# An attention stage: the values product is taken two query tiles after the scores, spare score banks hold some projections, and the engines' orders are rewritten

## The reference

```
q_latent, kv_latent = x @ wq_down, x @ wkv_down          # ranks 192 and 64
q = [q_latent @ wq_nope, rope(q_latent @ wq_rope)]       # 16 heads, 128 + 64 wide
k = [kv_latent @ wk_nope, rope(kv_latent @ wk_rope)]
v = (kv_latent @ wv_up).reshape(b, t, 16, 192)
scores = einsum('bthd,bshd->bhts', q, k) / sqrt(192)     # causal mask, then softmax
out = einsum('bhts,bshd->bthd', softmax(scores), v).reshape(b, t, 16 * 192) @ wo
```

## Time and profile before

| | us |
|---|---|
| median of 3 runs (1310.30 to 1316.01) | 1311.97 |
| the profiled execution, its own time | 1314.4 |
| its span, first to last instruction | 1312.6 |
| PE / DVE / ACT / POOL busy over the span | 1161.8 / 720.3 / 646.2 / 493.9 |

### The profile page before, as it was taken

How to read it: one execution, slowest core, us unless ns; L and a number is a source line. 1 busy time by engine, 2 the same in 40 slices (tenths; PEclk the granted TensorE clock), 3 DMA queues, 4 the chain that set the end, 5 groups by cost and what they waited for, 6 DMA issues and landing times. The chain is left out here.

```text
span 1312.6 us, 23292 instructions
## 1 busy us (share of the span) xinstructions
PE 1161.8 (89%) x7616; PEld 936.2 (71%) x7616; DVE 720.3 (55%) x1298; ACT 646.2 (49%) x1287; POOL 493.9 (38%) x386
## 2 busy tenths in 40 slices
PE   6678889888888898898888988998999999999997
PEld 3456667667677676676776766776788887888886
DVE  6556756556555556565555565554444445444444
ACT  3545556555555565555555555664433333333332
POOL 1263534543444445335444453421333332333332
PEclk9989999999999999999999999998999999999999
DMA  5001001000000000100000000103633333533332
GB/s 194 33 0 32 1 1 32 1 0 26 5 0 2 28 0 0 31 0 0 31 0 0 15 0 1 57 25 97 198 112 115 112 114 107 143 114 111 113 112 88
DMA packets 26304, 67.35 MB, mean 51 GB/s; under 512 B 3029, under 2 KB 9557, under 8 KB 26265
## 3 DMA queue, kind: packets, MB, share of 16 engines
q1 hardware_dynamic: 26120, 66.78, 16.6%
q10 hardware_dynamic: 144, 0.07, 0.0%
HBM read 62.36 MB, written 4.47 MB: 51 GB/s over the span
## 5 line engine op out<-in xcount | busy, mean ns | idle before, releaser
L714 ACT ACTIVATE prob<-ps_s,nm 128x128 f32<-128x128 f32 (+7 forms) x256 | 189.5, 740 | 203.3 <-DVE nm L866 200.9
L1305 POOL TENSOR_TENSOR hl<-hf,hh 128x512 fp32r<-128x512 f32 x96 | 123.5, 1286 | 294.9 <-ACT hh L1242 294.9
L866 DVE TENSOR_REDUCE nm<-ps_s 128x1 f32<-128x128 f32 (+7 forms) x256 | 192.3, 751 | 70.5 <-PE ps_s L548 69.0
L571 PE MATMUL ps_o<-pt,kvn 128*64 128x128 f32 x2304 | 154.0, 277 | 64.5 <-DVE pt L875 49.5
L571 PEld LDWEIGHTS ps_o<-pt,kvn 128*64 128x64 f32 x2304 | 126.2, 136 | 100.9 <-ACT pt L724 51.2
L559 PE MATMUL ps_t<-ident,prob 128*128 128x128 f32 x1152 | 173.0, 276 | 9.4 <-DVE pt L875 6.7
L1017 POOL TENSOR_TENSOR xtf<-xtf,sinv 128x512 f32<-128x512 f32 x62 | 79.4, 1280 | 223.4 <-DVE xtf L835 221.2
L559 PEld LDWEIGHTS ps_t<-ident,prob 128*128 128x128 f32 x1152 | 138.7, 142 | 32.2 <-issue 10.9
L1032 POOL TENSOR_TENSOR qlo<-t,qhi 64x512 fp32r<-64x512 f32 x64 | 82.0, 1281 | 159.8 <-ACT qhi L751 147.2
L724 ACT ACTIVATE pt<-ps_t 128x128 f32<-128x128 f32 (+2 forms) x192 | 96.6, 503 | 88.1 <-PE ps_t L559 86.7
L875 DVE COPY pt<-ps_t 128x128 f32<-128x128 f32 (+2 forms) x192 | 101.6, 529 | 56.2 <-PE ps_t L559 55.3
(11 more groups left out here) (272 smaller groups left out, 2689.5 us busy)
## 6 DMA issues: line engine op xcount, KB each, us to landing
routing<-wT_scratch SPq DMA_DIRECT2D x34, 256.0 KB, 3.7
raw_a<-in_e SPq DMA_DIRECT2D x17, 384.0 KB, 3.1
cosv<-in_e SPq DMA_DIRECT2D x17, 384.0 KB, 3.1
sinv<-wT_scratch SPq DMA_DIRECT2D x17, 384.0 KB, 3.6
raw<-in_e SPq DMA_DIRECT2D x17, 384.0 KB, 3.0
routing<-wT_scratch SPq DMA_DIRECT2D x16, 384.0 KB, 3.3
raw_a<-in_a SPq DMA_DIRECT2D x8, 512.0 KB, 3.3
raw_b<-in_b SPq DMA_DIRECT2D x8, 480.0 KB, 3.9
```

The lines of the kernel that those rows point to most:

```text
L571: mm = nc.tensor.matmul(ps_o[64 * e:64 * e + 64, at], kvn[:, b * 8 + j, :], pt[t % 2][:, e, j, :], start=j == 0, stop=j == t)
L714: nc.scalar.activation(prob[t % 2][e][:, 0:len(halves) * width].rearrange("p (h k) -> p h k", k=width), ps_s[e][:, 0:len(halves), 0:width] ...
L866: nc.vector.tensor_reduce(out=nm[:, e:e + 1], in_=ps_s[e][:, 0:len(halves), 0:halves[0][1]], axis=AXXY, op=ALU.max, negate=True).then_inc( ...
L1305: nc.gpsimd.tensor_tensor(hl[:, c, :], hf[:, c, :], hh[:, c, :].bitcast(F32), ALU.subtract).then_inc(h_lo, 1)
```

## The change

PE takes V(t-2) in tile t where it took V(t-1). The lists of all four engines are rewritten around that. Lp and QR1 go to the second bank of head 0, and KR0 and KR1 to that of head 1 (`SPARE`), while tiles 0 to 3 leave these banks free; a later S(4,e) waits until DVE has read QR1 or KR1 there. The others stay in `ps_x`. Lp moves from tile 0 to tile 1, KR1 from 5 to 3, L0 from 4 to 5, Yp1 from 6 to 4, QL1 from the end of 5 into 6 ahead of V(4), B from the end of 6 to that of 5, WA from 7 to the end of 6. On POOL the difference pass of KR0 (L1032) now stands behind `out_low` of the round's first half, and that of KR1 still ends the round; ACT rounds KR1's rotated part (`rope_hi` with `which`) only in tile 1 of the next round. The amount of work is the same. Parts that only rename or pass a bank along are left out.

```diff
-STAGE = ["Lp", "QR0", "KR0", "QL0", "QR1", "L0", "Yp0", "KR1", "QL1", "Yp1", "B", "WA", "Y0", "Y1"]
+STAGE = ["QR0", "Lp", "KR0", "QL0", "QR1", "KR1", "Yp0", "Yp1", "L0", "B", "QL1", "WA", "Y0", "Y1"]
+TURNS = {"QR0": "W0", "KR0": "W1", "QL0": "W2", "QR1": "W3"}
+SPARE = {"Lp": 0, "QR1": 0, "W3": 0, "KR0": 1, "KR1": 1, "W1": 1}
...
+            return ps_s[SPARE[name]][:, 1, :] if name in SPARE else ps_x
...
-                return a_split, (0 if b is None else i + 1) * 4 + 4
+                return a_split, (0 if b is None else i + 1) * 4 + 2
...
+                if t == TPC and half == 1:
+                    held = ("KR1" if e else "QR1") if not is_last(i, b) else "W1" if e else "W3"
+                    pe.wait_ge(*consumed(i, b, held))
...
                         if t == 0:
                             scores(i, b, t, 0, 0)
-                            if has:
-                                turn(sp, tp, 0, 0)
-                                turn(sp, tp, 0, 1)
+                            turns(0)
+                            products()
                             scores(i, b, t, 1, 0)
+                            turns(1)
+                            also("QR0")
+                        elif t == 1:
+                            scores(i, b, t, 0, 0)
+                            products()
                             also("Lp")
...
+                            turns(0)
+                            turns(1)
+                            scores(i, b, t, 1, 0)
+                            also("KR0")
                         elif t < TPC:
                             scores(i, b, t, 0, 0)
-                            turn(sp, tp, 0, 0)
-                            turn(sp, tp, 1, 0)
+                            turns(0)
+                            also("QL0" if t == 2 else "QR1")
+                            products()
+                            turns(1)
                             scores(i, b, t, 1, 0)
-                            values(sp, bp, tp)
-                            also(("KR0", "QL0", "QR1")[t - 1])
+                            if t == 3:
+                                also("KR1")
                         elif t == TPC:
                             scores(i, b, t, 0, 0)
-                            turn(sp, tp, 0, 0)
                             scores(i, b, t, 0, 1)
-                            also("L0")
-                            turn(sp, tp, 1, 0)
+                            turns(0)
+                            also("Yp0")
+                            products()
+                            turns(1)
                             scores(i, b, t, 1, 0)
                             scores(i, b, t, 1, 1)
-                            values(sp, bp, tp)
-                            also("Yp0")
+                            also("Yp1")
                         else:
                             scores(i, b, t, 0, 0)
                             turn(sp, tp, 0, 0)
                             scores(i, b, t, 0, 1)
                             turn(sp, tp, 0, 1)
-                            also(("KR1", "Yp1", "WA")[t - TPC - 1])
-                            scores(i, b, t, 1, 0)
-                            turn(sp, tp, 1, 0)
-                            turn(sp, tp, 1, 1)
-                            scores(i, b, t, 1, 1)
+                            if t < TILES - 1:
+                                also(("L0", "QL1")[t - TPC - 1])
+                            products()
                             if t == TILES - 1:
                                 also("Y0")
-                            values(sp, bp, tp)
-                            also(("QL1", "B", "Y1")[t - TPC - 1])
+                            scores(i, b, t, 1, 0)
+                            turns(1)
+                            scores(i, b, t, 1, 1)
+                            also(("B", "WA", "Y1")[t - TPC - 1])
...
-                        rope_low(s + 1, 0, 1 - b, (rope_sum, s * 4 + 7))
-                        rope_low(s + 1, 1, 1 - b, (rope_sum, s * 4 + 7))
                         rope_sum_of(s + 1, 3)
+                        rope_low(s + 1, 0, 1 - b, (rope_sum, s * 4 + 8))
...
                     out_low(s, 0)
                     if more:
+                        rope_low(s + 1, 1, 1 - b, (olo_done, s * 2 + 1))
                         rope_low(s + 1, 2, 1 - b, (olo_done, s * 2 + 1))
                         rope_low(s + 1, 3, 1 - b, (olo_done, s * 2 + 1))
```

More of the change, by code:

```diff
@@ L332, in misc_predecessor @@
 def misc_predecessor(i, b, name):
[L334 to L340, removed]
+    spare = SPARE.get(name)
+    order = FIRST if isinstance(i, int) and i == 0 else LAST if isinstance(i, int) and i == PAIRS - 1 else LATER
+    if spare is not None:
+        earlier = [x for x in order[:order.index((b, name))] if x[0] == b and SPARE.get(x[1]) == spare]
+        return (i, *earlier[-1]) if earlier else None
+    earlier = [x for x in order[:order.index((b, name))] if x[1] not in SPARE]
+    if earlier:
+        return (i, *earlier[-1])
+    return (0, None, PROLOGUE[-1]) if isinstance(i, int) and i == 0 else (i - 1, *LATER[-1])
 def halves_of(t):
@@ L637, in body, with turns, products @@
                     for t in range(TILES):
-                        sp, bp, tp = before_tile(i, b, t)
-                        has = earlier or t > 0
+                        sp, _, tp = before_tile(i, b, t)
+                        def turns(e):
+                            if earlier or t > 0:
+                                for g in range(len(groups_of(tp))):
+                                    turn(sp, tp, e, g)
+                        def products():
+                            if earlier or t > 1:
+                                values(*before_tile(i, b, t, 2))
@@ L688, in _ @@
             s, t = 2 * PAIRS - 1, TILES - 1
-            for e in range(2):
-                for g in range(2):
-                    turn(s, t, e, g)
+            for g in range(2):
+                turn(s, t, 0, g)
+            values(s, 1, t - 1)
+            for g in range(2):
+                turn(s, t, 1, g)
             pe.wait_ge(widened, s * 2 + 2)
@@ L912, in body @@
                         has = earlier or t > 0
+                        if more and t == 1:
+                            rope_products(i, b, "QR0", s + 1)
+                        if more and t == 2:
+                            rope_products(i, b, "KR0", s + 1)
+                        if more and t == 3:
+                            latent_low(i, b, 0, s + 1, 1 - b)
+                        if more and t == TPC:
+                            rope_products(i, b, "KR1", s + 1)
+                        if t == TPC + 1 and earlier:
+                            add_out(misc(i, b, "Yp1"), ps_x, s - 1, 1 - b, 1, 1)
@@ L913, in body @@
+                        if t == TPC + 2 and b == 0:
+                            split_b(i, b)
+                        if t == TPC + 3 and b == 0 and not is_last(i):
+                            split_a(i, b, i + 1)
+                        maximum(s, t, 0)
+                        if has and (t == 0 or t > TPC):
+                            take_turned(sp, tp, 0, 1)
                         if t == 0 and earlier:
                             invert(s - 1, 1)
+                        if more and t == 3:
+                            rope_products(i, b, "QR1", s + 1)
@@ L929, in body @@
-                        if more and t == TPC + 1:
-                            rope_products(i, b, "KR1", s + 1)
-                        if t == TPC + 2 and earlier:
-                            add_out(misc(i, b, "Yp1"), ps_x, s - 1, 1 - b, 1, 1)
-                        if t == TPC + 3 and b == 0 and not is_last(i):
-                            split_a(i, b, i + 1)
-                        if has and t > TPC:
-                            take_turned(sp, tp, 1, 1)
-                        maximum(s, t, 1)
```

143 lines of the change are left out of this document (70 added, 73 removed).

## The result

The changed kernel takes 1193.26 us (median; 1190.07 to 1212.5), the kernel before 1311.13 on the same chip. The ratio is 0.909, with a 95% interval of 0.905 to 0.913; ratios leave out executions in a second, slower state, such as the one at 1212.5 here. The forecast was 1203, within 1180 to 1252. The profiled execution took 1190.85, its span is 1189.0.

A forecast was written before the change was run, and what follows sets the result against it. PE was held by late results, its waits worth 131 us; less 22 us left or new, 109 gained: 1205.4 in the profiled run's terms, 1203 in the median's. Forecast range 1180 to 1228 (0.68), wider range 1180 to 1252.

The forecast's parts named there:

- The bound and the floor: PE in attention rounds: late results, not engine time, bound it; all waits worth 131 us, floor 1183 in the profiled run.
- sign of being wrong: PE's busy time in a round not the same as before, or waits left over 4 us a round.
- V, spreads, Yp1: PE's waits for transposed copies, ACT's filling and QL1's bank all go: 75.4, 28.0 and 13.9 us.
- Transposes: PE's waits for copies to leave banks: of 13.8 us, 0.2 a round stays, at T(6,0) in tile 7.
- Tight places: S(4,0) fits with 0.4 us to spare, S(3,0) comes 0.3 late a round, Yp0 fits with 1.2.
- the 6 us allowed for errors of these chains: Places with under 0.5 us to spare: 0.4 a round allowed, 6 us.
- WA: Behind QL1 in its bank: waits 0.8 us in each of eight b = 0 rounds, 6.4 us.
- First and last rounds: These rounds have lists of their own; 2 us kept for them.
- Heads of line: Rival: lists stall as a whole, tight places come late, 47 us in fifteen rounds, 1250; chance 0.21.
- the 2.98 us: DVE's idle time for ACT ahead of reading QL0, with C(2,1) said to be ready behind it.
- Waits that only move: Rival: V's waits return at S, only the spreads' and Yp1's go, 42 us, 1270; chance 0.05.
- wait of PE was for POOL: Rival: late `out_low` holds PE at Yp0 and POOL sets the round; 1335 at 10 us late; slower 0.04.

The follow-up runs named there:

- tuned_unrolled: Changed kernel with three small moves on ACT and DVE, and the loop over the six middle pairs of rounds written out; 1176.42 us, ratio 0.8949.
- tuned: Changed kernel with E(2,0) ahead of tile 2's rounding, QL1's reading ahead of E(6,0), two of the first four rotation differences on DVE; 1191.88 us, ratio 0.9087.
- late_latent: Changed kernel with ACT's reading of QL0 cut from two copies into sixteen small ones; 1204.73 us, ratio 0.9189.
- lag_one: Changed kernel with V(t-1) again at the end of tile t, only V(0) staying in tile 2; 1312.29 us, ratio 0.9999.
- before_lag_banks: Kernel before with V(t-2) in tile t and Lp, QR1 and KR0 in the spare banks, lists otherwise as before; 1304.73 us, ratio 0.9856.
- before_lag_two: Kernel before with V(t-2) right behind the first scores of tile t, banks and orders as before; 1275.56 us, ratio 0.9728.

## Why the prediction was right

- **The bound and the floor.** Right. All waits with 0.16 hidden in each were put at 131 us; taken from the fifteen rounds (780 less 131) that leaves 649, and *tuned_unrolled*, whose PE has hardly a gap left in its rounds, has 647.4 there. The 0.16 shows in the busy time too. PE's work in a b = 1 round is the same, and yet it is shown busy for 42.71 instead of 44.02; the 1.3 less stands beside the 1.4 a round that 142 waits of 0.16 make. So the prediction's sign of being wrong, a busy time that is not the same as before, was badly chosen: by its own account the busy time of before held parts of the waits.
- **V, spreads, Yp1.** Right in mechanism and size: 63.7, 23.5 and 11.7 us became 0.4, 0 and 0.
- **Transposes.** About right. In tile 7 T(6,0) is some 0.5 late where I kept 0.2; with 0.2 at S(3,0) for the 0.3 kept, the two are 0.6 net of a b = 1 round (42.96 against 42.38 in *tuned*), against 0.5.
- **Tight places.** S(4,0) was said to have 0.4 to spare, and had 0.4 (*late_latent*). That the figures agree so well is luck: from QL0's end PE took 6.2 to S(4,0), not 5.7, and the chain to the end of E(3,0) took 5.6 and 0.2 more to the score, not 5.3. Yp0 was said to have 1.2, and had 0.9. So the 6 us allowed for errors of these chains were not needed.
- **WA.** Mis-sized. I took 0.8 in eight rounds, 6.4. It is 0.6 late in six, and what *tuned* gained more in b = 0 rounds than in b = 1 (0.8 against 0.6) puts its price at some 0.2 a round, 1.3 in all: part of the delay would have been met elsewhere. With the 6 above, these 5.1 are some 11 of the 14 us by which the forecast of the fifteen rounds, 672, stood over the measured 658; this is the step that was off.
- **First and last rounds.** The 2 us kept are met by the 1.6 at W3, a wait that I had not seen.
- **Rivals.** Heads of line did not happen in the change, but it is what *lag_one* and *before_lag_banks* show, so its chance was fair: with the lag or the lists missing, the strict order on DVE gives the waits back. One reading offered for it was wrong: C(2,1) was not ready during the 2.98 us. Its transposes began at 449.40 and the step behind them came at 450.06, when that idle time was over. Once ready it stood for some 2 us behind the two readings and M(3,0), so DVE did keep to the order of its list, but the 2.98 is not what this copy waited for. Waits that only move is what *before_lag_two* shows, at the side bank rather than at S. In the rounds of the change no wait of PE was for POOL but that of the first score.
- **What I got wrong** is the separate worth of the parts, in the expectations: 75.4 for the lag, 28.0 and 13.9 for the rest was a list of what goes when all goes, not a price of each.

## What to carry to other kernels

A list of waits tells what is gained if all the causes go at once; when one goes, the next wait in the same chain takes its place, so changes to lag, buffers and order are worth planning and measuring together. Chaining the lengths of rows from release to use gave spare times to within 0.4 us, which is enough to see which link to move next. When a change that shows in single rounds does not show in the total, compare the rounds one by one: what ate it may have nothing to do with it, as the loop's jump here.

## What the runs showed of the hardware

- A loop's jump back stalled TensorE for 2.1 to 3.6 us at some jumps, each time with three instruction packets from 6.4 us ahead of the first score to 0.8 behind its start, and not at others, where there was one or none; written out, the same work had no such stall (rounds of 44.2 and 42.3 each time in *tuned_unrolled*).
- After such an idle stretch PE ran for a while at a lower granted clock: 0.65 over 4.9 us in *tuned*. In *before_lag_banks*, after the stall of 2.87 us at the jump ahead of round 8 (the columns are those of the stretches above):

```profile
480.00:484.00 4.00, 0.97 (x3) 0.49 (x4) 0.95 (x3) 3.78 (x7) 1.93 (x2) 0.73 0.02 4
484.00:488.00 4.00, 3.04 (x22) 2.53 (x24) 0.29 (x1) 0.00 (x0) 3.13 (x3) 0.50 0.02 4
488.00:492.00 4.00, 4.00 (x27) 3.60 (x24) 0.62 (x1) 0.95 (x3) 0.00 (x0) 0.50 0.02 4
```

  0.50 is the lower of the clock's two levels, 1.2 GHz of 2.4. The round that ended with the stall took 51.1 instead of 48.1, and the one behind it 54.3 instead of 49.8, with a stop of 0.95 in it that no view explains: the stall of 3 us went with a loss of over 7.
- ACT's small copies in a row overlap: sixteen of 64 elements, shown at 0.22 each, took 1.99 together, 0.12 apiece.
